# A softmax whose shift runs on ScalarE and whose exponential is taken after the transpose

## The chip, the cores and the metric

One core of a Trainium2 chip runs the whole program. The metric is the device time in microseconds (us), the median of three runs. Five engines work side by side and meet through semaphores: TensorE (PE, with its weight loads as PEld), VectorE (DVE), ScalarE (ACT), GpSimd (POOL) and SyncE (SP), which here only issues DMAs. Each engine takes its instructions in the order in which they are written.

## The reference

128 sequences of 128 rows of width 256 go through one gated block: cross-attention with 16 heads of width 16, then a feed-forward part whose activations are quantised per row.

```python
q, k, v = heads(layernorm(x) @ Wq.T + bq), heads(ctx @ Wk.T + bk), heads(ctx @ Wv.T + bv)
scores  = q @ k.T / sqrt(16)                 # per head, 128 x 128, masked above the diagonal
weights = softmax(scores, axis=-1)
x = x + tanh(g_xattn) * ((weights @ v) @ Wo.T + bo)
x = x + tanh(g_ffn) * bitlinear(silu(bitlinear(layernorm(x), w_gate)) * bitlinear(layernorm(x), w_up), w_down)
```

The change concerns the softmax alone: exp(score - row maximum) in 16 heads, and its transposition, since the product with v needs the keys on the partitions.

## The kernel before, in words

A tile is one sequence. The loop runs over pairs of sequences, each pair in two sections, `c.s == 0` (the even tile) and `c.s == 1` (the odd tile). A section works on four tiles at once, in four stages: attention of tile t, output projection of t-1 (`outp`), feed-forward of t-2 (`ffn`), down projection of t-3 (`down`); beside them the inputs of the next pair are projected (`proj`: k in the even section, q and v in the odd one). Each engine has its own `body(c)`, in which the order of its work is written out by hand for the two sections; `walk` calls it for 67 pairs of sections, of which 62 have every stage. `c.tile(n)` and `c.pair(n)` are the semaphore values of n tiles or pairs back.

Attention runs in two halves of eight heads. Half 0 lives in PSUM banks 0 and 1 (`S_B[0]`), half 1 in banks 2 and 3 (`S_B[1]`), each 128 queries by 1024 columns (8 heads of 128 keys). For each half of a tile:

- `scores` (TensorE, L499 to L510): six matmuls of 512 columns write the masked scores. They wait for `p_ok` of the tile before.
- `top` (VectorE, L845 to L851): a row maximum per head, negated, into `row_max`.
- Half 0: `shift` (VectorE, L853 to L857) adds `row_max` to the eight heads in one instruction and writes `prob` in SBUF; `exp` (ScalarE, L706 to L712) then takes the exponential of the 1024 columns in SBUF, in place.
- Half 1: `exp` (ScalarE, L714 to L719) takes the exponential straight out of PSUM, one instruction per head, with the head's `row_max` as bias.
- `probs_t` (TensorE, L512 to L516): eight transposes of `prob` back into the same banks.
- `probs_out` (ScalarE, L721 to L725): one copy of 1024 columns from PSUM to `prob_t` in SBUF, which releases `p_ok`.
- `values` (TensorE, L518 to L528): 16 matmuls with v; v has a column of ones, so that the sum of each row's exponentials comes with them. `out_natural` (L530, L859) transposes the result back and divides by that sum.

Other work that shares the engines and that the steps of the prediction name: the hidden transposes (L611) and ScalarE's `h_t` out of them (L768); ScalarE's `o_t` (L736) and VectorE's rest of it; the two gate/up halves (TensorE L597 to L609, where the second waits for `h_ok[0]`), ScalarE's `tanh` for each (L727 to L732), VectorE's `gu` and `h` (`gated`, L868 to L876); the output projection (L542 to L552); VectorE's `y` (L944); ScalarE's bias of k or q (L750) and `q_high` (L757); the maximum over the hidden row (L919). ScalarE's order in the odd section is `exp(1)`, `tanh(0)`, `exp(0)`, q, `probs_out(0)`, `tanh(1)`, `probs_out(1)`; in the even one `exp(0)`, `tanh(0)`, `exp(1)`, `probs_out(0)`, `tanh(1)`, k, `probs_out(1)`.

Of the kernel before, what the change touches and what calls it, by code (L numbers as in the profile page):

```python
# [12 lines left out]
P = 128  # L13
# [11 lines left out]
def flamingo_block(nc, x, ctx_in, g_x, g_f, wq, bq, wk, bk, wv, bv, wo, bo, w_gate, w_up, w_down, out):  # L25
# [15 lines left out]
    with es:  # L41
# [59 lines left out]
        prob = sb("prob", [P, HEADS, P])  # L101
# [256 lines left out]
        s_sub = sem("s_sub")  # L358
        s_exp = [sem("s_exp0"), sem("s_exp1")]
# [85 lines left out]
        with nc.Block() as block:  # L445
# [52 lines left out]
            def _(pe):  # L498
# [13 lines left out]
                def probs_t(c, half):  # L512
                    pe.wait_ge(s_exp[half], c.tile(0))
                    for n in range(HPC):
                        last = nc.tensor.transpose(S_B[half][:, n * P:(n + 1) * P], prob[:, HPC * half + n, :], ident[:, :])  # L515
                    last.then_inc(p_tr[half], 1)  # L516
# [117 lines left out]
                def body(c):  # L634
                    if c.s == 0:
# [18 lines left out]
                        if c.attn:  # L654
                            probs_t(c, 0)
# [6 lines left out]
                        if c.attn:  # L662
                            probs_t(c, 1)
# [5 lines left out]
                    else:  # L669
# [20 lines left out]
                        if c.attn:  # L690
                            probs_t(c, 1)
                            probs_t(c, 0)
# [12 lines left out]
            def _(act):  # L705
                def exp(c, half):  # L706
                    if half == 0:

                        act.wait_ge(s_sub, c.tile(0))
                        v = prob[:, 0:HPC, :]  # L710
                        nc.scalar.activation(v, v, ACT.Exp).then_inc(s_exp[0], 1)  # L711
                        return  # L712

                    act.wait_ge(s_max[1], c.tile(0))  # L714
                    wait(act, p_tr[1], c.tile(1))
                    for n in range(HPC):
                        last = nc.scalar.activation(prob[:, HPC + n, :], S_B[1][:, n * P:(n + 1) * P], ACT.Exp,  # L717
                                                    bias=row_max[:, HPC + n:HPC + n + 1])
                    last.then_inc(s_exp[1], 1)  # L719

                def probs_out(c, half):  # L721
                    act.wait_ge(p_tr[half], c.tile(0))
                    wait(act, pv_mm[half], c.tile(1))
                    nc.scalar.copy(prob_t[:, HPC * half:HPC * (half + 1), :].rearrange("p h k -> p (h k)"),  # L724
                                   S_B[half]).then_inc(p_ok[half], 1)  # L725
# [60 lines left out]
                def body(c):  # L786
                    if c.s == 0:
# [8 lines left out]
                        if c.attn:  # L796
                            exp(c, 0)
                        if c.ffn:
                            tanh(c, 0)
                        if c.attn:  # L800
                            exp(c, 1)
                            probs_out(c, 0)
# [4 lines left out]
                        if c.attn:  # L807
                            probs_out(c, 1)
# [335 lines left out]
```

## Time and profile before

| | |
|---|---|
| median of 3 runs | 1931.26 us (1930.18 to 1932.64) |
| the profiled execution, its own time | 1932.1 us |
| its span, first to last instruction | 1930.4 us |
| TensorE, matmuls | 1747.9 us busy, 91% |
| TensorE, weight loads | 1396.7 us, 72% |
| VectorE | 1658.1 us, 86%, 3609 instructions |
| ScalarE | 1434.1 us, 74%, 2897 instructions |
| GpSimd | 1053.1 us, 55% |
| TensorE's granted clock, mean | 0.99 of full speed |
| DMA | 91.22 MB, 47 GB/s |

Busy time is the union of an engine's instructions, so a share of 91% still has small gaps. A timeline line gives start, duration, engine, line of the kernel, operation, output <- input, the number of merged instructions, and in brackets the idle time of the engine before it with what ended it. In a group line "us, mean ns | idle before" is the busy total, the mean duration of one, and the idle time just before the group. Instructions of one engine overlap a little: the next starts before the recorded end of the one before it.

### The profile page before, as it was taken

To read this page: it belongs to the slowest core of one execution; us is meant where nothing else is said; L and a number is where in the kernel's file an instruction comes from. 1 tells how busy PE (TensorE), PEld (TensorE's weight loads), DVE (VectorE), ACT (ScalarE), POOL (GpSimd) and SP (SyncE) were. 2 spreads that over 40 slices of the span, in tenths; PEclk is the share of its full clock that TensorE was granted. 3 is DMA by queue.
4 is the path that set the end of the run, shared out by engine and by line. 5 is a ranking of instruction groups with operands and counts; after the bars stand their busy time and mean duration, and the time that the engine had idled before them with its cause. 6 is when DMAs were issued, how large, how long until landed. Compare 5 with 4: busy or idle time off the path is not lost. (4 is left out here: it accounts for less than half of the span.)

```text
span 1930.4 us, 46249 instructions
## 1 busy us (share of the span) xinstructions
PE 1747.9 (91%) x15430; PEld 1396.7 (72%) x15430; DVE 1658.1 (86%) x3609; ACT 1434.1 (74%) x2897; POOL 1053.1 (55%) x1623
## 2 busy tenths in 40 slices
PE   3799999999999999999999999999999999999984
PEld 2677777777777777777777777777777777777762
DVE  4588988988988888888898898898898898898884
ACT  3577777787777787777777777777777777778772
POOL 4455555556556556555555555555555555655641
PEclk9999999999999999999999999999999999999996
DMA  3222122122122122122122222222212212212210
GB/s 106 45 53 44 43 53 46 42 55 49 37 56 48 37 57 48 38 55 48 40 52 48 43 50 50 44 47 53 42 46 53 43 45 53 50 38 56 48 20 11
DMA packets 131900, 91.22 MB, mean 47 GB/s; under 512 B 13521, under 2 KB 131409, under 8 KB 131665
## 3 DMA queue, kind: packets, MB, share of 16 engines
q1 hardware_dynamic: 130416, 88.13, 22.4%
q8 instruction: 126, 2.06, 0.4%
q14 instruction: 110, 0.89, 0.2%
q10 hardware_dynamic: 1248, 0.14, 0.1%
HBM read 37.88 MB, written 16.78 MB: 28 GB/s over the span
## 5 line engine op out<-in xcount | busy, mean ns | idle before, releaser
L507 PE MATMUL psum<-k_blk,q_t 128*128 128x512 f32 x1536 | 419.1, 408 | 1.2 <-DVE q_t L935 1.2
L1041 POOL TENSOR_SCALAR xc<-x,ln 128x256 f32<-128x256 f32 x128 | 61.3, 479 | 485.5 <-DVE ln L898 485.5
L849 DVE TENSOR_REDUCE row_max<-psum 128x8 f32<-128x1024 f32 x256 | 311.2, 1215 | 7.1 <-PE psum L507 6.9
L507 PEld LDWEIGHTS psum<-k_blk,q_t 128*128 128x128 f32 x1536 | 268.8, 188 | 62.1 <-issue 14.1
L717 ACT ACTIVATE prob<-psum,row_max 128x128 f32<-128x128 f32 x1024 | 277.4, 385 | 12.7 <-DVE row_max L849 12.6
L1064 POOL TENSOR_SCALAR hq<-h,sm 128x1024 f16<-128x1024 f32 x128 | 143.2, 1119 | 226.6 <-DVE sm L929 220.5
L724 ACT COPY prob_t<-psum 128x1024 f32<-128x1024 f32 x256 | 262.4, 1025 | 5.1 <-PE psum L515 1.4
L515 PE MATMUL psum<-ident,prob 128*128 128x128 f32 x2048 | 255.1, 273 | 4.4 <-ACT prob L711 3.9
L515 PEld LDWEIGHTS psum<-ident,prob 128*128 128x128 f32 x2048 | 228.8, 141 | 6.6 <-ACT prob L711 5.1
L732 ACT ACTIVATE th<-psum,sm 128x512 f32<-128x512 f32 x256 | 178.8, 698 | 14.9 <-PE psum L607 13.2
L872 DVE SCALAR_TENSOR_TENSOR gu<-th,psum 128x512 f32<-128x512 f32 x256 | 174.9, 683 | 10.9 <-ACT th L732 6.8
L876 DVE TENSOR_TENSOR h<-gu,psum 128x512 f32<-128x512 f32 x256 | 175.9, 687 | 8.8
L773 ACT COPY o_raw<-psum 128x512 f32<-128x512 f32 x128 | 75.1, 587 | 139.4 <-PE psum L526 139.4
L607 PE MATMUL psum<-wg_t,xq_t 128*128 128x512 f16 x512 | 155.0, 385 | 21.7 <-DVE h L876 20.5
L526 PE MATMUL psum<-prob_t,v_sb 128*32 128x128 f32 x4096 | 151.6, 277 | 19.0 <-ACT prob_t L724 19.0
L768 ACT ACTIVATE h_t<-psum 128x1024 f16<-128x1024 f16 x128 | 131.0, 1023 | 41.0 <-PE psum L614 39.6
L856 DVE TENSOR_TENSOR prob<-psum,row_max 128x1024 f32<-128x1024 f32 x128 | 155.6, 1216 | 2.2
L919 DVE TENSOR_REDUCE sm<-h 128x1 f32<-128x1024 f32 x128 | 155.5, 1215 | 2.2
L711 ACT ACTIVATE prob<-prob 128x1024 f32<-128x1024 f32 x128 | 139.2, 1087 | 20.9 <-DVE prob L856 20.9
L607 PE MATMUL psum<-wu_t,xq_t 128*128 128x512 f16 x512 | 153.7, 382 | 0.0
L624 PE MATMUL psum<-wd_t,h_t 128*128 128x256 f16 x1024 | 135.9, 277 | 18.3 <-ACT h_t L768 18.3
L526 PEld LDWEIGHTS psum<-prob_t,v_sb 128*32 128x32 f32 x4096 | 100.2, 109 | 68.3 <-ACT prob_t L724 35.5
(116 smaller groups left out, 3729.9 us busy)
## 6 DMA issues: line engine op xcount, KB each, us to landing
k_blk<-k_t SPq DMA_DIRECT2D x512, 64.0 KB, 2.4
c_in<-in_ctx SPq DMA_DIRECT2D x64, 256.0 KB
x_in<-in_x SPq DMA_DIRECT2D x64, 256.0 KB
out<-y SPq DMA_DIRECT2D x128, 128.0 KB
g_nat<-in_L_ffn_w_gate SPq DMA_DIRECT2D x1, 1024.0 KB, 10.5
g_nat<-in_L_ffn_w_up SPq DMA_DIRECT2D x1, 1024.0 KB, 12.8
g_nat<-in_L_ffn_w_down SPq DMA_DIRECT2D x1, 1024.0 KB, 14.4
w_nat<-in_L_xattn_Wq SPq DMA_DIRECT2D x1, 256.0 KB, 4.1
```

The source lines that it names most:

```text
L507: last = nc.tensor.matmul(dst, q_t[:, b, a, half, c.s, :], k_blk[:, w, half, c.s, 4 * b:4 * b + 4, :], start=n == 0, stop=n == len(TERMS) - 1)
L515: last = nc.tensor.transpose(S_B[half][:, n * P:(n + 1) * P], prob[:, HPC * half + n, :], ident[:, :])
L526: last = nc.tensor.matmul(B6[VW * j:VW * (j + 1), g * P:(g + 1) * P], v_sb[:, c.s, n, :], prob_t[:, n, :], start=True, stop=True)
L607: last = nc.tensor.matmul(dst, xq_t[:, ic, :], w[:, ic, half * HALF:(half + 1) * HALF], start=ic == 0, stop=ic == DC - 1)
L717: last = nc.scalar.activation(prob[:, HPC + n, :], S_B[1][:, n * P:(n + 1) * P], ACT.Exp, bias=row_max[:, HPC + n:HPC + n + 1])
L724: nc.scalar.copy(prob_t[:, HPC * half:HPC * (half + 1), :].rearrange("p h k -> p (h k)"), S_B[half]).then_inc(p_ok[half], 1)
L732: nc.scalar.activation(th[:, half, :], GATE, ACT.Tanh, scale=row(sm, c.s, G_FACTOR)).then_inc(th_ok[half], 1)
L849: nc.vector.tensor_reduce(out=row_max[:, HPC * half:HPC * (half + 1)], in_=S_B[half].rearrange("p (h k) -> p h k", k=P), axis=AX.X, op=ALU ...
L856: nc.vector.tensor_tensor(prob[:, 0:HPC, :], S_B[0].rearrange("p (h k) -> p h k", k=P), row_max[:, 0:HPC].unsqueeze(2).to_broadcast((P, HP ...
L872: nc.vector.scalar_tensor_tensor(out=gu[:, half, :], in0=th[:, half, :], scalar=1.0, in1=UP, op0=ALU.add, op1=ALU.mult).then_inc(gu_ok[hal ...
L876: nc.vector.tensor_tensor(h[:, half, :], gu[:, half, :], GATE, ALU.mult).then_inc(h_ok[half], 1)
L919: nc.vector.tensor_reduce(out=row(sm, t, H_MAX), in_=h[:, :, :].rearrange("p a b -> p (a b)"), axis=AX.X, op=ALU.max, apply_absolute_value ...
```

## The change

VectorE's add leaves, and ScalarE adds the row maximum in both halves, one Identity instruction per head with the head's `row_max` as bias, from PSUM into `s_low` (the former `prob`). TensorE transposes these shifted scores. The exponential is then the instruction that takes the transposed 1024 columns out of PSUM into `prob_t`, where a copy stood. ScalarE's order becomes, even section: shift 0, tanh 0, shift 1, exponential 0, tanh 1, k, exponential 1; odd section: shift 0, tanh 0, shift 1, q, `q_high`, exponential 0, tanh 1, exponential 1. In the odd section the halves were taken as 1, 0 and are now taken as 0, 1.

```diff
--- before.py
+++ after.py
@@ -98,7 +98,7 @@
         k_t = sb("k_t", [P, 2, DC, 2, P], F32R)
         k_blk = sb("k_blk", [P, 2, DC, 2, HPC, P], F32R)
         v_sb = sb("v_sb", [P, 2, HEADS, VW])
-        prob = sb("prob", [P, HEADS, P])
+        s_low = sb("s_low", [P, HEADS, P])
         prob_t = sb("prob_t", [P, HEADS, P])
         o_raw = sb("o_raw", [P, 4 * P])
         o_n = sb("o_n", [P, D])
@@ -355,8 +355,7 @@
 
         s_mm = [sem("s_mm0"), sem("s_mm1")]
         s_max = [sem("s_max0"), sem("s_max1")]
-        s_sub = sem("s_sub")
-        s_exp = [sem("s_exp0"), sem("s_exp1")]
+        s_sub = [sem("s_sub0"), sem("s_sub1")]
         p_tr = [sem("p_tr0"), sem("p_tr1")]
         p_ok = [sem("p_ok0"), sem("p_ok1")]
         pv_mm = [sem("pv_mm0"), sem("pv_mm1")]
@@ -509,10 +508,10 @@
                                                     start=n == 0, stop=n == len(TERMS) - 1)
                     last.then_inc(s_mm[half], 1)
 
-                def probs_t(c, half):
-                    pe.wait_ge(s_exp[half], c.tile(0))
+                def shifted_t(c, half):
+                    pe.wait_ge(s_sub[half], c.tile(0))
                     for n in range(HPC):
-                        last = nc.tensor.transpose(S_B[half][:, n * P:(n + 1) * P], prob[:, HPC * half + n, :], ident[:, :])
+                        last = nc.tensor.transpose(S_B[half][:, n * P:(n + 1) * P], s_low[:, HPC * half + n, :], ident[:, :])
                     last.then_inc(p_tr[half], 1)
 
                 def values(c, half):
@@ -652,7 +651,7 @@
                         if c.down:
                             down(c)
                         if c.attn:
-                            probs_t(c, 0)
+                            shifted_t(c, 0)
                         if c.outp:
                             out_proj(c)
                         if c.ffn:
@@ -660,7 +659,7 @@
                         if c.proj:
                             project_qk(c)
                         if c.attn:
-                            probs_t(c, 1)
+                            shifted_t(c, 1)
                         if c.next.attn:
                             scores(c.next, 0)
                         if c.attn:
@@ -688,8 +687,8 @@
                         if c.proj:
                             project_qk(c)
                         if c.attn:
-                            probs_t(c, 1)
-                            probs_t(c, 0)
+                            shifted_t(c, 0)
+                            shifted_t(c, 1)
                         if c.ffn:
                             gate_up(c, 1)
                         if c.proj:
@@ -703,26 +702,20 @@
 
             @block.scalar
             def _(act):
+                def shift(c, half):
+                    act.wait_ge(s_max[half], c.tile(0))
+                    wait(act, p_tr[half], c.tile(1))
+                    for n in range(HPC):
+                        at = HPC * half + n
+                        last = nc.scalar.activation(s_low[:, at, :], S_B[half][:, n * P:(n + 1) * P], ACT.Identity,
+                                                    bias=row_max[:, at:at + 1])
+                    last.then_inc(s_sub[half], 1)
+
                 def exp(c, half):
-                    if half == 0:
-
-                        act.wait_ge(s_sub, c.tile(0))
-                        v = prob[:, 0:HPC, :]
-                        nc.scalar.activation(v, v, ACT.Exp).then_inc(s_exp[0], 1)
-                        return
-
-                    act.wait_ge(s_max[1], c.tile(0))
-                    wait(act, p_tr[1], c.tile(1))
-                    for n in range(HPC):
-                        last = nc.scalar.activation(prob[:, HPC + n, :], S_B[1][:, n * P:(n + 1) * P], ACT.Exp,
-                                                    bias=row_max[:, HPC + n:HPC + n + 1])
-                    last.then_inc(s_exp[1], 1)
-
-                def probs_out(c, half):
                     act.wait_ge(p_tr[half], c.tile(0))
                     wait(act, pv_mm[half], c.tile(1))
-                    nc.scalar.copy(prob_t[:, HPC * half:HPC * (half + 1), :].rearrange("p h k -> p (h k)"),
-                                   S_B[half]).then_inc(p_ok[half], 1)
+                    nc.scalar.activation(prob_t[:, HPC * half:HPC * (half + 1), :].rearrange("p h k -> p (h k)"),
+                                         S_B[half], ACT.Exp).then_inc(p_ok[half], 1)
 
                 def tanh(c, half):
                     act.wait_ge(gu_mm[half], c.tile(2))
@@ -794,18 +787,18 @@
                         if c.outp:
                             out_t(c)
                         if c.attn:
+                            shift(c, 0)
+                        if c.ffn:
+                            tanh(c, 0)
+                        if c.attn:
+                            shift(c, 1)
                             exp(c, 0)
                         if c.ffn:
-                            tanh(c, 0)
+                            tanh(c, 1)
+                        if c.proj:
+                            project_qk(c)
                         if c.attn:
                             exp(c, 1)
-                            probs_out(c, 0)
-                        if c.ffn:
-                            tanh(c, 1)
-                        if c.proj:
-                            project_qk(c)
-                        if c.attn:
-                            probs_out(c, 1)
                             values(c)
                             keep_residual(c)
                     else:
@@ -818,20 +811,20 @@
                         if c.outp:
                             out_t(c)
                         if c.attn:
-                            exp(c, 1)
+                            shift(c, 0)
                         if c.ffn:
                             tanh(c, 0)
                         if c.attn:
-                            exp(c, 0)
+                            shift(c, 1)
                         if c.proj:
                             project_qk(c)
                             q_high(c)
                         if c.attn:
-                            probs_out(c, 0)
+                            exp(c, 0)
                         if c.ffn:
                             tanh(c, 1)
                         if c.attn:
-                            probs_out(c, 1)
+                            exp(c, 1)
                             values(c)
                         if c.proj:
                             project_v(c)
@@ -845,16 +838,10 @@
                 def top(c, half):
 
                     dve.wait_ge(s_mm[half], c.tile(0))
-                    wait(dve, s_exp[1] if half == 1 else s_sub, c.tile(1))
+                    wait(dve, s_sub[half], c.tile(1))
                     nc.vector.tensor_reduce(out=row_max[:, HPC * half:HPC * (half + 1)],
                                             in_=S_B[half].rearrange("p (h k) -> p h k", k=P), axis=AX.X,
                                             op=ALU.max, negate=True).then_inc(s_max[half], 1)
-
-                def shift(c):
-                    dve.wait_ge(s_max[0], c.tile(0))
-                    wait(dve, p_tr[0], c.tile(1))
-                    nc.vector.tensor_tensor(prob[:, 0:HPC, :], S_B[0].rearrange("p (h k) -> p h k", k=P),
-                                            row_max[:, 0:HPC].unsqueeze(2).to_broadcast((P, HPC, P)), ALU.add).then_inc(s_sub, 1)
 
                 def out_natural(c):
                     dve.wait_ge(on_tr, c.tile(1))
@@ -969,7 +956,6 @@
                         if c.proj:
                             norm_stats(c)
                         if c.attn:
-                            shift(c)
                             top(c, 1)
                         if c.outp:
                             out_t(c)
@@ -990,7 +976,6 @@
                     else:
                         if c.attn:
                             top(c, 0)
-                            shift(c)
                         if c.outp:
                             out_natural(c)
                         if c.attn:
```

## Rows read from the trace of the kernel before

**Rows 1.** Busy time by stage: window, us, busy (instructions) per engine, clock, DMA

```profile
999.90:1028.60 28.70, 26.87 (x240) 21.56 (x240) 25.54 (x57) 22.16 (x45) 16.24 (x25) 1.00 0.24 47
```

**Rows 2.** Waits of TensorE over the span: us in total, times, longest

```profile
PE psum L607 <- DVE h L876: 20.5, 65, 2.2
PE psum L526 <- ACT prob_t L724: 19.0, 66, 0.8
```

**Rows 3.** Timeline, even tile of a steady pair: start, duration, engine, line

```profile
999.94 0.64 PE L526 MATMUL psum<-prob_t,v_sb 128*32 128x128 f32 x16 [0.28 <-ACT prob_t L724]
...
1003.27 1.21 DVE L849 TENSOR_REDUCE row_max<-psum 128x8 f32<-128x1024 f32 x1
...
1005.64 0.37 ACT L736 CAST o_t<-psum 128x256 fp32r<-128x256 f32 x1
...
1007.26 0.67 ACT L732 ACTIVATE th<-psum,sm 128x512 f32<-128x512 f32 x1
...
1007.72 1.04 PE L515 MATMUL psum<-ident,prob 128*128 128x128 f32 x8
...
1007.92 0.48 DVE L944 SCALAR_TENSOR_TENSOR y<-psum,sm,x 128x256 f32<-128x256 f32 x1 [0.20 <-PE psum L624]
1008.32 0.68 DVE L872 SCALAR_TENSOR_TENSOR gu<-th,psum 128x512 f32<-128x512 f32 x1
...
1008.55 0.94 PE L549 MATMUL psum<-w_t,o_t 128*128 128x256 f32 x6
...
1009.78 0.61 PE L607 MATMUL psum<-wg_t,xq_t 128*128 128x512 f16 x2 [0.28 <-DVE h L876]
...
1010.86 0.69 ACT L732 ACTIVATE th<-psum,sm 128x512 f32<-128x512 f32 x1
```

**Rows 4.** Timeline, odd tile of the same pair

```profile
1018.59 1.02 ACT L768 ACTIVATE h_t<-psum 128x1024 f16<-128x1024 f16 x1 [0.25 <-PE psum L614]
...
1019.51 0.37 ACT L736 CAST o_t<-psum 128x256 fp32r<-128x256 f32 x1
...
1020.07 2.17 ACT L717 ACTIVATE prob<-psum,row_max 128x128 f32<-128x128 f32 x8 [0.19 <-DVE row_max L849]
...
1022.08 0.74 ACT L732 ACTIVATE th<-psum,sm 128x512 f32<-128x512 f32 x1
...
1023.77 0.84 ACT L750 ACTIVATE q_f<-psum,bq_c 128x256 f32<-128x256 f32 x2
...
1024.64 1.26 ACT L757 CAST q_t<-q_f 64x512 fp32r<-64x512 f32 x2
...
1025.92 1.02 ACT L724 COPY prob_t<-psum 128x1024 f32<-128x1024 f32 x1
...
1026.97 0.69 ACT L732 ACTIVATE th<-psum,sm 128x512 f32<-128x512 f32 x1
...
1027.55 1.00 ACT L724 COPY prob_t<-psum 128x1024 f32<-128x1024 f32 x1
...
1028.61 0.64 PE L526 MATMUL psum<-prob_t,v_sb 128*32 128x128 f32 x16 [0.28 <-ACT prob_t L724]
```

**Rows 5.** Groups of instructions by line and form: busy us, mean ns, idle before

```profile
L717 ACT ACTIVATE prob<-psum,row_max 128x128 f32<-128x128 f32 x1024 | 277.4, 385 | 12.7 <-DVE row_max L849 12.6
...
L724 ACT COPY prob_t<-psum 128x1024 f32<-128x1024 f32 x256 | 262.4, 1025 | 5.1 <-PE psum L515 1.4
...
L856 DVE TENSOR_TENSOR prob<-psum,row_max 128x1024 f32<-128x1024 f32 x128 | 155.6, 1216 | 2.2
...
L711 ACT ACTIVATE prob<-prob 128x1024 f32<-128x1024 f32 x128 | 139.2, 1087 | 20.9 <-DVE prob L856 20.9
```

**Rows 6.** Timeline, VectorE and TensorE at the start of the odd tile

```profile
1015.81 1.22 DVE L849 TENSOR_REDUCE row_max<-psum 128x8 f32<-128x1024 f32 x1
...
1017.51 0.60 PE L533 MATMUL psum<-ident,o_raw 128*128 128x128 f32 x4
...
1018.20 0.25 DVE L862 RECIPROCAL row_rcp<-psum 128x16 f32<-128x16 f32 x1
```

More of the change, by code:

```diff
@@ L820, in body @@
                         if c.attn:
-                            exp(c, 1)
+                            shift(c, 0)
                         if c.ffn:
@@ L824, in body @@
                         if c.attn:
-                            exp(c, 0)
+                            shift(c, 1)
                         if c.proj:
@@ L829, in body @@
                         if c.attn:
-                            probs_out(c, 0)
+                            exp(c, 0)
                         if c.ffn:
@@ L833, in body @@
                         if c.attn:
-                            probs_out(c, 1)
+                            exp(c, 1)
                             values(c)
```

## The prediction

> **What bounds the kernel now.** I read the stage table of one steady pair of sequences first: in a window of 28.70 us TensorE is busy for 26.87, VectorE for 25.54, ScalarE for 22.16 and GpSimd for 16.24; TensorE's clock is at its full 2.4 GHz level (granted 1.00) [rows 1]. So TensorE sets the pace, with 1.8 us of idle time per pair, and a change can gain no more than that unless it removes TensorE work; this one removes none (16 score transposes per tile before and after). Then the waits: two of TensorE's gaps end with an engine that the change touches. It waits 20.5 us in all, 65 times, for VectorE's `h` before the second gate/up half, and 19.0 us, 66 times, for ScalarE's `prob_t` before the value matmuls [rows 2], 0.3 us each time. Last the timeline of that pair, even tile [rows 3] and odd tile [rows 4]; the pair lasts 28.67 us, from one launch of the last value matmuls at 999.94 to the next at 1028.61. What it shows: the engine with the largest share is not the one that ends every stage. In the second half of the odd tile ScalarE works without a break from the exponential of 1020.07 to the copy that ends at 1028.55, and TensorE's last value matmuls start 0.06 us after it [rows 4].
>
> **What the change moves.** Per tile, VectorE loses one add of 1.22 us (L856) and ScalarE loses one exponential of 1.09 us (L711); the exponential of 8 x 128 columns with a bias column (L717, 8 in 2.17 us) becomes an Identity of the same form; ScalarE gains a second set of those eight; both PSUM copies (L724) become exponentials [rows 5]. Instructions on ScalarE: 11 per tile become 18. No DMA and no GpSimd instruction is added or moved. In the odd tile the order of the halves is swapped, for ScalarE's shifts and TensorE's transposes alike.
>
> Prices. **Eight shifts**: 2.17 us, since L717 is the same form (128x128 out of PSUM, a bias column), with another function. That Identity is not much cheaper: two Identities of 256 columns with a bias column start 0.37 us apart (0.84 us for both, less 0.47), and eight exponentials of 128 columns 0.255 us apart ((2.17 - 0.385) / 7) [rows 4, 5]. A column costs 0.855 ns by the 1024-column copy against the 0.37 us, 256-column one ((1025 - 370) / 768) [rows 4, 5], so 128 columns fewer make the Identity's step 0.37 - 0.11 = 0.26 us. Ends: 2.07 and 2.27 us. **Exponential of 1024 columns out of PSUM**: not in the trace; ends are the PSUM copy, 1.025, and the exponential out of SBUF, 1.087 [rows 5]. I take 1.04, nearer the copy, since source and columns are the same and only the function differs.
>
> The Trainium skill, "ScalarE: Activation LUTs", section "What ACT_TABLE_LOAD costs", gives an ACTIVATE with a bias pointer about 280 ns + 0.833 ns per column, and an overlap of 93 ns between neighbours. For 128 columns that is 387 ns, and the trace agrees with 385; for eight, though, it is 2.44 us where the trace has 2.17, and the sum below would become +1.78 us per pair instead of +0.97. I follow the trace. The Trainium skill, the same page's section "Rules for kernel authors", puts an add on VectorE, not ScalarE, which speaks against this change; the trace agrees (1.22 us there, 2.17 here).
>
> **VectorE's gain.** 1.22 us per tile goes from an engine that has 3.1 us idle per pair. In the odd tile the add is followed by L862, which starts at 1018.20 and also needs the transposes of L533, which end at 1018.11: without the add it could start about 0.05 us sooner at most [rows 6]. In the even tile the following row maximum waits for the score matmuls anyway. I cost the removal at nothing; what covers it is TensorE's own order.
>
> **Even tile.** ScalarE issues the next instruction about 0.10 us before the recorded end of its predecessor (1018.59 + 1.02 - 0.10 = 1019.51) [rows 4], and 0.16 us before the end of a set of eight (1020.07 + 2.17 - 0.16 = 1022.08). After `o_t` (1005.64, 0.37 us) the first shift starts at 1005.91 and ends at 1008.08, because the row maximum, done at 1004.48, is long there. The tanh behind it starts at 1007.92 instead of 1007.26 and ends at 1008.59. VectorE's L872 started at 1008.32, held by L944 until 1008.40; now it is held by the tanh and starts at 1008.62 (a hand-over of 0.03): **+0.30 us**. Then `h` and the second gate/up matmuls, already waiting for it at 1009.78, go to 1010.08. The transposes on the way start at 1008.14 instead of 1007.72, and the output projection behind them ends at about 1009.91 instead of 1009.49: under 1010.08, so the tanh decides [rows 3]. The shift of half 1 (1008.49 to 1010.66) and exponential 0 (from 1010.50) are done before TensorE needs them; the second tanh starts at about 1011.57. From there TensorE has no break until its hidden transposes of the odd tile, and the +0.30 travels on.
>
> **Odd tile.** `h_t` waits for those transposes, so `o_t` is at 1019.51 + 0.30 = 1019.81, and then ScalarE never waits: shift 0 starts at 1020.08; tanh 0 at 1022.09 (+2.01); shift 1 at 1022.67 (+0.58, as 1026.97 to 1027.55), ends 1024.84; q bias at 1024.68; q high at 1025.55 (+0.87, as 1023.77 to 1024.64); exponential 0 at 1026.83 (+1.28, as 1024.64 to 1025.92); tanh 1 at 1027.90 (+1.05 for the copy, +0.02 for the function); exponential 1 at 1028.48, ends 1029.52. TensorE's last value matmuls follow 0.06 later, at 1029.58 instead of 1028.61 [rows 4]: **+0.97 us for the pair**, 0.30 of the even and 0.67 of the odd tile. On the way the transposes of half 1, which can't start before shift 1 ends at 1024.84, may hold TensorE for a moment; that is swallowed by the later wait. The wait for `prob_t` grows from 0.28 us to at most 0.28 + 0.67 = 0.95.
>
> **Sum.** 62 pairs run with all stages in, 62 x 0.97 = +60 us. In the first and last pair the feed-forward or the projections are missing and ScalarE has room; from row maximum to `p_ok` the work of a half is no longer than before (2.17 against 1.22 + 1.09), so I add nothing. The profiled execution took 1932.1 us with a span of 1930.4; it becomes 1992. It stood 0.8 us above the median of the three runs, 1931.26, so I predict **1991 us**, +3.1%. Each 0.1 us on a set of eight counts three times per pair (once even, twice odd), 19 us in all; the exponential's far end, 1.087, adds 0.05 twice, 6 us.
>
> **Rivals.**
> - *The even tile's delay does not come, or the shifts are a little cheap.* With sets at 2.07 us, +0.67 x 62 = 42: 1973 us. For it: Identity is another function than the one measured. Against: the 0.26 us step above. Chance 0.13.
> - *VectorE becomes late behind the second tanh.* In the even tile tanh 1 slips by 0.71 (1010.86 as it was, 1011.57 now), with it `gu`, `h`, the hidden maximum, and the odd tile's first row maximum, L849, from 1015.81 to 1016.52. If this reached TensorE in full in place of 0.30, the pair would grow by 1.38 us: +86, 2017 us. Against: that row maximum ends at 1017.74, and L862 behind it must wait for transposes that end at 1018.41, so 0.67 us of slack is left; the add's removal is what makes the room [rows 6]. Chance 0.09.
> - *Not slower: Identity is cheap enough.* The place is ScalarE's chain in the odd tile. It decides at a set of 1.83 us (0.67 = 2 x 0.335 saved), a step of 0.206 us instead of 0.255. Below 1.70 us the old 0.28 us wait for `prob_t` vanishes as well, and then -0.28 x 62 = -17: 1914 us. Against: the Identities of L750 show no such speed. Chance 0.07 for this side together.
> - That the change does not do what it says is excluded by its text: the add is gone from VectorE's order, and both halves take the same path.
>
> **Chances and range.** A measurement of this kernel can tell about 0.2% (4 us) from no change. Forecast 0.71, smaller loss 0.13, VectorE late 0.09, not slower 0.07, of which faster 0.05 and within the bound 0.02. So slower by over 0.2%: 0.93. The forecast's own range is 1979 to 1999 (sets of 2.12 to 2.19 us, exponentials of 1.025 to 1.087). With the smaller loss and half of the larger one the range becomes 1972 to 2008.
>
> **What would show it.** Right: in the changed profile, ScalarE's sets of eight at 2.1 to 2.2 us, twice per tile; 1024-column exponentials out of PSUM at 1.03 to 1.09 us; TensorE's wait for `prob_t` at 0.7 to 0.95 us in each pair, some 50 us in all, and its wait for `h` at 0.3 to 0.5; VectorE's idle time up by over 3 us per pair; a pair of 29.6 us. Wrong: a pair of 28.7 us or less; no growth of the wait for `prob_t`; a new wait of TensorE for `o_n`, `hq` or `xq`, which would mean that VectorE's chain counts; or Identities 0.2 us apart.

## The result and the profile after

| | before | after |
|---|---|---|
| median | 1931.4 us | 1991.45 us (1990.44 to 1993.63) |
| ratio to before, 95% interval | | 1.0311 (1.0298 to 1.0323) |
| span of the profiled execution | 1930.4 us | 1990.2 us |
| a pair, median between launches of L533/L532 two apart | 28.70 us | 29.68 us |
| of it from the even tile's launch to the odd one's, and back | 15.52, 13.18 us | 15.77, 13.91 us |
| instructions of ScalarE, of VectorE | 2897, 3609 | 3793, 3481 |

The change costs 3.1%: 60 us, or 0.98 us for each of the 62 full pairs. Line numbers after are one lower on TensorE's side and 7 to 15 lower behind it (L525 is the old L526, L514 the old L515, L606 the old L607; L710 is the shift, L717 the exponential out of PSUM, L725 the tanh, L842 the row maximum, L849 the old L862).

The stage table of a steady pair after, with the columns of [rows 1]:

```profile
999.90:1029.60 29.70, 27.20 (x240) 21.52 (x240) 23.57 (x55) 24.05 (x60) 16.40 (x25) 1.00 0.22 46
```

Against [rows 1] ScalarE is 1.9 us busier and VectorE 2.0 us less. TensorE's idle time in the window is 2.50 us, of 1.83 before. VectorE's goes from 3.2 to 6.1 us. The engine that was relieved is not the one that the pair waits for.

TensorE's waits over the span, after:

```profile
PE psum L525 <- ACT prob_t L717: 48.8, 65, 1.1
PE psum L565 <- ACT xq_t L776: 35.1, 62, 0.6
PE psum L538 <- DVE o_n L852: 25.3, 65, 1.0
...
PE psum L514 <- ACT s_low L710: 20.1, 66, 1.6
PE psum L606 <- DVE h L863: 16.2, 64, 2.2
```

Against [rows 2] the wait for `prob_t` grew by 30 us and a wait for the shifted scores appeared, 20 us; the wait for `h` did not grow, it fell by 4. The three waits that grew most all end with ScalarE (the third is the one for `h_t`, 18.3 to 22.3 us over the span); the one for VectorE's `o_n` fell from 29.8 to 25.3.

The timeline of the even tile after, to be laid beside [rows 3] (this pair starts 0.10 us later, 1000.04 for 999.94):

```profile
1000.04 0.65 PE L525 MATMUL psum<-prob_t,v_sb 128*32 128x128 f32 x16 [0.75 <-ACT prob_t L717]
...
1005.66 0.37 ACT L729 CAST o_t<-psum 128x256 fp32r<-128x256 f32 x1
...
1005.91 2.19 ACT L710 ACTIVATE s_low<-psum,row_max 128x128 f32<-128x128 f32 x8
...
1007.92 0.76 ACT L725 ACTIVATE th<-psum,sm 128x512 f32<-128x512 f32 x1
...
1008.15 1.09 PE L514 MATMUL psum<-ident,s_low 128*128 128x128 f32 x8 [0.26 <-ACT s_low L710]
...
1008.71 0.69 DVE L859 SCALAR_TENSOR_TENSOR gu<-th,psum 128x512 f32<-128x512 f32 x1 [0.29 <-ACT th L725]
...
1010.18 0.60 PE L606 MATMUL psum<-wg_t,xq_t 128*128 128x512 f16 x2 [0.22 <-DVE h L863]
```

The shift starts when `o_t` is out of the way, at 1005.91, and the tanh follows at 1007.92, where it was at 1007.26. The transposes wait 0.26 us for the shift, `gu` 0.29 us for the tanh, and the second gate/up half starts at 1010.18, or 1010.08 without the offset, 0.30 us later than before. The offset is not constant, though: at the hidden transposes it has shrunk to 0.02 us (L613 at 1004.09, L614 before at 1004.07), so between them and the gate/up half the even tile loses 0.38 us.

The odd tile after, beside [rows 4]:

```profile
1019.91 0.37 ACT L729 CAST o_t<-psum 128x256 fp32r<-128x256 f32 x1
...
1020.16 2.19 ACT L710 ACTIVATE s_low<-psum,row_max 128x128 f32<-128x128 f32 x8
...
1022.17 0.76 ACT L725 ACTIVATE th<-psum,sm 128x512 f32<-128x512 f32 x1
...
1022.74 2.25 ACT L710 ACTIVATE s_low<-psum,row_max 128x128 f32<-128x128 f32 x8
...
1024.74 0.99 ACT L743 ACTIVATE q_f<-psum,bq_c 128x256 f32<-128x256 f32 x2
...
1025.76 1.26 ACT L750 CAST q_t<-q_f 64x512 fp32r<-64x512 f32 x2
...
1027.04 1.03 ACT L717 ACTIVATE prob_t<-psum 128x1024 f32<-128x1024 f32 x1
...
1028.09 0.69 ACT L725 ACTIVATE th<-psum,sm 128x512 f32<-128x512 f32 x1
...
1028.68 1.01 ACT L717 ACTIVATE prob_t<-psum 128x1024 f32<-128x1024 f32 x1
...
1029.75 0.65 PE L525 MATMUL psum<-prob_t,v_sb 128*32 128x128 f32 x16 [0.76 <-ACT prob_t L717]
```

ScalarE has no idle time in this stretch. Its q bias starts at 1024.74 where TensorE's projection was ready at 1024.14; in [rows 4] it started at 1023.77. Everything behind it is late, and TensorE waits 0.76 us for the last `prob_t`, 0.28 before.

The groups of instructions that the change made, after:

```profile
L710 ACT ACTIVATE s_low<-psum,row_max 128x128 f32<-128x128 f32 x2048 | 567.6, 439 | 0.1
...
L717 ACT ACTIVATE prob_t<-psum 128x1024 f32<-128x1024 f32 x256 | 271.4, 1061 | 3.7
...
L725 ACT ACTIVATE th<-psum,sm 128x512 f32<-128x512 f32 x256 | 194.9, 761 | 15.7 <-PE psum L606 14.1
```

### The profile page after: what moved, and what is told of

Its sections match the earlier page's. It is cut to its first block and busy times, and to the rows that moved or that the text cites. A ratio compares the mean times of both kernels' runs of the same rounds, so it can differ in the third digit from the quotient of the medians.

```text
span 1990.2 us, 47017 instructions
## 1 busy us (share of the span) xinstructions
PE 1765.1 (89%) x15430; PEld 1392.2 (70%) x15430; DVE 1527.0 (77%) x3481; ACT 1555.7 (78%) x3793; POOL 1063.8 (53%) x1623
## 5 line engine op out<-in xcount | busy, mean ns | idle before, releaser
L710 ACT ACTIVATE s_low<-psum,row_max 128x128 f32<-128x128 f32 x2048 | 567.6, 439 | 0.1
L842 DVE TENSOR_REDUCE row_max<-psum 128x8 f32<-128x1024 f32 x256 | 311.6, 1217 | 64.4 <-PE psum L506 64.3
L514 PE MATMUL psum<-ident,s_low 128*128 128x128 f32 x2048 | 272.0, 276 | 21.8 <-ACT s_low L710 20.1
L717 ACT ACTIVATE prob_t<-psum 128x1024 f32<-128x1024 f32 x256 | 271.4, 1061 | 3.7
L514 PEld LDWEIGHTS psum<-ident,s_low 128*128 128x128 f32 x2048 | 224.7, 141 | 55.1 <-ACT s_low L710 54.8
L725 ACT ACTIVATE th<-psum,sm 128x512 f32<-128x512 f32 x256 | 194.9, 761 | 15.7 <-PE psum L606 14.1
L525 PE MATMUL psum<-prob_t,v_sb 128*32 128x128 f32 x4096 | 151.6, 277 | 48.8 <-ACT prob_t L717 48.8
L606 PE MATMUL psum<-wg_t,xq_t 128*128 128x512 f16 x512 | 155.0, 385 | 17.4 <-DVE h L863 16.2
L525 PEld LDWEIGHTS psum<-prob_t,v_sb 128*32 128x32 f32 x4096 | 100.1, 109 | 98.0 <-ACT prob_t L717 65.3
L623 PE MATMUL psum<-wd_t,h_t 128*128 128x256 f16 x1024 | 136.0, 277 | 22.3 <-ACT h_t L761 22.3
L606 PE MATMUL psum<-wu_t,xq_t 128*128 128x512 f16 x512 | 153.5, 382 | 0.0
L623 PEld LDWEIGHTS psum<-wd_t,h_t 128*128 128x128 f16 x1024 | 95.9, 99 | 62.5 <-ACT h_t L761 37.7
L922 DVE TENSOR_TENSOR q_t<-q_f,q_t 64x512 fp32r<-64x512 f32 x128 | 99.2, 775 | 37.4 <-ACT q_t L750 35.2
```

Of the source, the lines that this page charges most:

```text
L525: last = nc.tensor.matmul(B6[VW * j:VW * (j + 1), g * P:(g + 1) * P], v_sb[:, c.s, n, :], prob_t[:, n, :], start=True, stop=True)
L606: last = nc.tensor.matmul(dst, xq_t[:, ic, :], w[:, ic, half * HALF:(half + 1) * HALF], start=ic == 0, stop=ic == DC - 1)
L623: last = nc.tensor.matmul(DOWN, h_t[:, k * P:(k + 1) * P], wd_t[:, k, :], start=k == 0, stop=k == IC - 1)
L710: last = nc.scalar.activation(s_low[:, at, :], S_B[half][:, n * P:(n + 1) * P], ACT.Identity, bias=row_max[:, at:at + 1])
L717: nc.scalar.activation(prob_t[:, HPC * half:HPC * (half + 1), :].rearrange("p h k -> p (h k)"), S_B[half], ACT.Exp).then_inc(p_ok[half], 1)
L725: nc.scalar.activation(th[:, half, :], GATE, ACT.Tanh, scale=row(sm, c.s, G_FACTOR)).then_inc(th_ok[half], 1)
```

## The experiments

Eight of them price a part of the change, three look for a faster version. Each is compared with the kernel before on its own chip; where a difference counts, I take ratios.

**1. half1_only: the later exponential, by itself.**

```diff
-    last = nc.scalar.activation(prob[:, HPC + n, :], S_B[1][...], ACT.Exp, bias=...)
+    last = nc.scalar.activation(prob[:, HPC + n, :], S_B[1][...], ACT.Identity, bias=...)
...
-    nc.scalar.copy(prob_t[...], S_B[half])
+    nc.scalar.activation(prob_t[...], S_B[half], ACT.Exp if half == 1 else ACT.Copy)
```

> The kernel before, with half 1 alone changed: its eight ScalarE instructions per tile become Identity, and its exponential is taken on the way out of PSUM, in place of the copy. Half 0 stays as before. My theory: an Identity of 128 columns with a bias column costs what the exponential did (a set of eight 2.17 us, as after, 2.19), and an exponential of 1024 columns out of PSUM costs what the copy did (1.02 to 1.03 us in the trace of after, where it does not overlap a set). So nothing moves: 1931 us, within 4. Rival, the function itself costs: an exponential out of PSUM as dear as the one out of SBUF (1.09 us) would lengthen the odd tile's last ScalarE instruction by 0.06 us, 62 times, 1935 us; a cheaper Identity would bring the time below 1925.

Measured: 1931.62 us, ratio 1.0002 (0.9993 to 1.0011). ScalarE's groups:

```profile
L717 ACT ACTIVATE prob<-psum,row_max 128x128 f32<-128x128 f32 x1024 | 277.5, 386 | 12.7 <-DVE row_max L849 12.7
L724 ACT ACTIVATE prob_t<-psum 128x1024 f32<-128x1024 f32 x256 | 265.5, 1037 | 5.1 <-PE psum L515 1.4
```

Identity takes 386 ns as the exponential did (385, [rows 5]), and the mixed group of copies and exponentials 1037 ns for 1025. Moving the exponential of half 1 behind the transpose costs nothing.

**2. dve_add: the exponential behind the transpose in both halves, VectorE keeps the add.**

```diff
 # half1_only, and for half 0:
-    nc.scalar.activation(v, v, ACT.Exp).then_inc(s_exp[0], 1)      # exp(c, 0), gone
-    pe.wait_ge(s_exp[half], c.tile(0))
+    pe.wait_ge(s_exp[1] if half == 1 else s_sub, c.tile(0))
-    ... ACT.Exp if half == 1 else ACT.Copy)
+    ... ACT.Exp)
```

> The same as half1_only, and half 0 too is exponentiated on the way out; but the row maximum of half 0 is still added by VectorE, in one instruction, as in the kernel before, and ScalarE's exponential of 1.09 us per tile goes. ScalarE's and TensorE's order stay those of before. My theory (ScalarE's chain in the odd tile ends the pair, and the loss came from the second set of eight): ScalarE is done 1.0 us sooner in the odd tile, so TensorE's 0.28 us wait for prob_t goes, and nothing else on the path: 62 x 0.28 = 17 us, 1914 us (1910 to 1920). The even tile keeps its wait for h, since VectorE's y comes before it. Rival, taking the exponential after the transpose is itself what costs (a later release of the banks): slower than 1931 us.

Measured: 1931.77 us, ratio 1.0001 (0.9992 to 1.0010). ScalarE does 1.09 us less per tile and the time is the same. My forecast of a 17 us gain fell. The odd tile of this kernel, ScalarE and the last value matmuls:

```profile
1020.06 2.17 ACT L710 ACTIVATE prob<-psum,row_max 128x128 f32<-128x128 f32 x8 [0.18 <-DVE row_max L838]
...
1022.08 0.74 ACT L725 ACTIVATE th<-psum,sm 128x512 f32<-128x512 f32 x1
...
1023.78 0.84 ACT L743 ACTIVATE q_f<-psum,bq_c 128x256 f32<-128x256 f32 x2 [0.97 <-PE psum L579]
...
1025.93 1.03 ACT L717 ACTIVATE prob_t<-psum 128x1024 f32<-128x1024 f32 x1
...
1027.57 1.02 ACT L717 ACTIVATE prob_t<-psum 128x1024 f32<-128x1024 f32 x1
...
1028.64 0.65 PE L526 MATMUL psum<-prob_t,v_sb 128*32 128x128 f32 x16 [0.30 <-ACT prob_t L717]
```

The q bias has 0.97 us of idle time before it and starts at 1023.78, as in [rows 4]: it waits for TensorE's projection, which ends at 1023.75. In the kernel before, ScalarE's exponential of half 0 and TensorE's projection ended within 0.03 us of each other, at 1023.76 and 1023.73:

```profile
1022.17 1.56 PE L579 MATMUL psum<-xn_t,w_t 128*128 128x256 f32 x12
...
1022.65 1.11 ACT L711 ACTIVATE prob<-prob 128x1024 f32<-128x1024 f32 x1
```

So its row looked like one chain without a break, while in its first half ScalarE was only level with TensorE: shortening that half gains nothing, and lengthening it by more than what little slack there is costs. What sets the last wait is the stretch from the q bias on (q, q high, exponential, tanh, exponential), whose length this change hardly touches. With both results, the step from before to dve_add costs nothing, and the whole loss comes with taking the add from VectorE to ScalarE (and with the new order of the halves, which experiment 4 prices).

**3. cheap_even, cheap_odd, cheap_both: the set of eight priced tile by tile.** One Identity of 1024 columns in place of each set of eight (the row maximum is not added in those tiles).

```diff
+    if c.s == 0:        # cheap_even; 1 for cheap_odd; no condition for cheap_both
+        nc.scalar.activation(s_low[:, HPC * half:HPC * (half + 1), :]..., S_B[half], ACT.Identity)
+        return
     for n in range(HPC):
```

> The changed kernel, in whose even tiles each set of eight shifts is one Identity of 1024 columns (1.0 us in place of 2.2). It leaves out the addition of the row maximum there. By my theory the even tile's share of the loss is 0.30 us per pair and goes, while 1.2 us per set are saved: the tanh is then no longer late and VectorE's y holds gu again, TensorE's 0.26 us wait for s_low goes and its wait for h is 0.28 again. 62 x 0.30 = 19: 1973 us (1969 to 1978). Rival, ScalarE's whole time counts: 2 x 1.2 x 62 = 149 us, 1843 us.

> The same in the odd tiles alone. ScalarE saves 2.3 us there. My theory as corrected by dve_add (in which ScalarE was done with its shifts 1 us early and the pair was no shorter, since its q bias then waits for TensorE's q projection and TensorE's last wait for prob_t stays 0.3 us): the odd tile returns to its state before the change and no further, 0.67 us per pair less, and the even tile's 0.30 stays: 1950 us (1945 to 1955). My theory as it was, in which a shorter ScalarE chain also removes the old 0.28 us wait: 1932 us.

> Both of the former: one Identity of 1024 columns in place of every set of eight, no addition of the row maximum. If the loss is the two shares and the rest of the change costs nothing (exponential on the way out, order of halves, the add gone from VectorE): 1931 us again (1928 to 1935), although ScalarE has 4.6 us per pair less to do than in the changed kernel and VectorE 2.4 less than before. Rival, a part of the loss is in the new order or in the later exponential: over 1937 us; a real gain from the relieved engines: under 1926 us.

Measured: cheap_even 1967.1 us, 1.0185 (1.0171 to 1.0199); cheap_odd 1955.4 us, 1.0124 (1.0110 to 1.0138); cheap_both 1930.1 us, 0.9991 (0.9982 to 1.0000). Pairs: 29.31, 29.08, 28.69 us. The two savings, 24 and 36 us, add up to the 60 us of the loss, and with both the changed kernel is back where the old one was. TensorE's waits in cheap_even, cheap_odd and cheap_both, in this order:

```profile
PE psum L525 <- ACT prob_t L721: 48.0, 64, 1.1
...
PE psum L606 <- DVE h L867: 20.5, 65, 2.2
```

```profile
PE psum L525 <- ACT prob_t L721: 19.1, 63, 1.1
PE psum L514 <- ACT s_low L714: 18.1, 64, 1.7
PE psum L606 <- DVE h L867: 17.0, 65, 2.2
```

```profile
PE psum L525 <- ACT prob_t L714: 19.1, 63, 1.1
...
PE psum L606 <- DVE h L860: 21.0, 65, 2.2
```

Each cure takes its own symptom: in the odd tile the `prob_t` wait falls from 48.8 to 19.1 us, in the even one the `s_low` wait falls out of the list and `h` is back at 20.5. That cheap_odd stops at 29.08 and not lower bears out what dve_add taught.

The single shares missed my bands by a little: even 0.37 us per pair, not 0.30, odd 0.60, not 0.67. The even share is larger because the tanh behind a set of eight takes longer than I had it (see the part on the sum below). The odd one is smaller because of a third wait, that of the weight load for the hidden transposes on GpSimd's `hq`, over the span; before, after, cheap_odd:

```profile
PEld psum L614 <- POOL hq L1064: 21.7, 63, 6.5
```

```profile
PEld psum L613 <- POOL hq L1049: 9.9, 6, 6.2
```

```profile
PEld psum L613 <- POOL hq L1053: 19.5, 52, 6.5
```

In the kernel before TensorE waits for `hq` in 63 places; after, TensorE is late by its own, and the wait is gone (6 left); cheap_odd brings it back 52 times (cheap_both 53, cheap_even 6). In steady pairs, from L532 to the matmuls of L613 it is 1.96 us after and 2.05 in cheap_odd (2.07 before). The odd tile's delay hides 0.1 us of the next even tile's work, and a removal of the former gives that back: the odd tile's own section gets 0.7 us shorter in cheap_odd (13.91 to 13.20), the next even one 0.1 us longer (15.77 to 15.87). The order in which the shares are taken doesn't matter: the even one is 0.37 us taken first (29.68 to 29.31) and 0.39 taken second (29.08 to 28.69), the odd one 0.60 and 0.62.

**4. odd_swap: the order of the halves in the odd tile as it was.**

```diff
-    shifted_t(c, 0)
-    shifted_t(c, 1)
+    shifted_t(c, 1)
+    shifted_t(c, 0)
... # and on ScalarE
-    shift(c, 0) ... tanh(c, 0) ... shift(c, 1)
+    shift(c, 1) ... tanh(c, 0) ... shift(c, 0)
```

> The changed kernel with the halves of the odd tile in the order 1, 0 again, for ScalarE's shifts and TensorE's transposes. My theory (ScalarE never waits in the odd tile after o_t, so that whatever delays its first shift delays the pair): the first shift then needs the row maximum of half 1, which ends at 1020.39 where ScalarE is free at 1020.16, and starts some 0.27 us later: 62 x 0.27 = 17 us, 2008 us (2003 to 2012). Rival, the order is indifferent because TensorE or VectorE ends the pair: 1991 us, within 4.

Measured: 2006.9 us, 1.0391 (1.0375 to 1.0407), within the forecast; a pair is 29.93 us, 0.25 longer. ScalarE's odd chain passes a later start straight on. The swap that the change made is worth about 15 us; without it the loss would be 76.

**5. dve_dummy and dve_odd_add: what VectorE's relief is worth.**

```diff
+    def dummy(c):                                    # dve_dummy, both tiles
+        nc.vector.tensor_tensor(spare, g_nat[:, 0, 0:1024]..., bo_eff[:, 0:HPC]..., ALU.add)
 # dve_odd_add, odd tile alone:
+        dve.wait_ge(s_max[0], c.tile(0))
+        dve.wait_ge(s_mm[1], c.tile(0))
+        nc.vector.tensor_tensor(spare, S_B[1]..., row_max[:, 0:HPC]..., ALU.add)
```

> The changed kernel with VectorE's 1.2 us given back: at the places where the shift stood, an add of the same 1024 columns on constants, which nobody waits for. If VectorE's relief is worth nothing, as I costed it: 1991 us, within 4. What the trace of after makes likelier: in the even tile nothing (0.9 us idle before the next row maximum, of 1.2, and slack behind it); in the odd tile VectorE has 0.83 us idle before L849, so o_n comes some 0.4 us later, its transposes and then ScalarE's o_t slip by 0.1 to 0.2 us, and ScalarE's chain with them: 1997 to 2004 us. Rival, VectorE's busy time counts in full: 2 x 1.2 x 62 = 149 us, 2140 us.

> The changed kernel with the very add that was removed (1024 columns out of PSUM plus the row maximum column, 1.22 us) put back on VectorE in the odd tile alone, at its old place between the first row maximum and L849; its result goes to a tile that nobody reads. dve_dummy left this open: its add read two SBUF operands, took 1.39 us, and GpSimd's small instruction beside it took 1.11 us in place of 0.26, after which TensorE's q projection waited 0.53 us for the split of xn. Theory by the trace of after: the row maximum ends at 1017.72, the add at 1018.9, L849 starts 0.3 us later than its 1018.55, o_n and its transposes too, and ScalarE's o_t slips by some 0.1 us: 62 x 0.1 = 6 us, 1997 us (1993 to 2002). If VectorE's relief is worth nothing: 1991, within 2. If what dve_dummy lost is VectorE's time and not GpSimd's: 2010.

Measured: dve_dummy 2010.8 us, 1.0410 (1.0395 to 1.0424); dve_odd_add 2009.7 us, 1.0394 (1.0377 to 1.0412), a pair 29.93 us. Both missed my bands. The second has an add of the real form (it reads the bank of half 1 and waits for those scores, which cost it 2.5 us in four places and nothing elsewhere), GpSimd is undisturbed, and it is one add per pair; still it costs 16 us (1.0394 less 1.0311), where I had expected 6; the 2010 us of its last rival, VectorE's time and not GpSimd's, is what came. Its waits of TensorE and its odd tile:

```profile
PE psum L539 <- DVE o_n L859: 47.3, 66, 1.1
PE psum L515 <- ACT s_low L711: 36.3, 126, 1.7
```

```profile
1024.39 1.21 DVE L843 TENSOR_REDUCE row_max<-psum 128x8 f32<-128x1024 f32 x1
...
1025.65 1.22 DVE L850 TENSOR_TENSOR spare<-psum,row_max 128x1024 f32<-128x1024 f32 x1
...
1026.79 0.25 DVE L856 RECIPROCAL row_rcp<-psum 128x16 f32<-128x16 f32 x1
...
1027.55 0.44 PE L539 MATMUL psum<-ident,o_n 128*128 128x128 f32 x2 [0.69 <-DVE o_n L859]
...
1028.02 0.37 ACT L730 CAST o_t<-psum 128x256 fp32r<-128x256 f32 x1
```

Behind the late first maximum (1024.39 to 1025.60) the add ends at 1026.87, the reciprocal (L856 of this kernel) and `o_n` follow, the wait for `o_n` goes from 25.3 to 47.3 us, and ScalarE's `o_t` starts 2.21 us after the launch of L533 (1025.81) instead of 2.00 (1017.91 to 1019.91). From there the odd chain carries the 0.2 us to the end, and TensorE meets it as a second wait for `s_low` in each pair (36.3 us for 20.1). So the removed add was worth 0.25 us per pair in the changed kernel. That it is worth this only because the second tanh has made VectorE late is read from the rows and no run separates it: with the add, the first maximum starts 1.42 us ahead of L533 here and 1.70 ahead in the kernel before (1015.81 and 1017.51, [rows 6]), where `o_t` still comes 2.00 us after L533 (1019.51, [rows 4]).

**6. early_half0 and scores_first: two tries at a faster version.**

```diff
 # early_half0, on dve_add, odd tile: TensorE           ScalarE
+    probs_t(c, 0)      # ahead of out_proj             # tanh 0, exponential 0, q, q_high,
     out_proj(c); project_qk(c); probs_t(c, 1)          # exponential 1, tanh 1
 # scores_first_add (on dve_add), scores_first_before (on before), TensorE, even tile
     quant_t(c)
+    scores(c, 1)
     inputs_t(c); out_t(c); hidden_t(c)
-    scores(c, 1)
```

> dve_add (VectorE adds for half 0, the exponential on the way out in both halves) with a new order in the odd tile: TensorE transposes half 0 ahead of the output projection, ScalarE takes exponential 0 ahead of q and exponential 1 ahead of the second tanh. In dve_add ScalarE is idle for 0.97 us before q, waiting for TensorE, and then does q, q high, exponential 0, tanh, exponential 1 in a row. If that row sets TensorE's last wait of the pair (0.30 us for prob_t): moving one exponential ahead of q removes it, 62 x 0.29 = 18: 1914 us (1910 to 1918). Rival, the time only moves on: the wait for prob_t goes and another wait of the pair (o_n, h_t, xq_t or h) grows by as much: 1931 us.

> dve_add with one step of TensorE's even tile moved: the scores of half 1 come right behind the transposes of xq, ahead of those of the inputs, of o_n and of the hidden row. They fill the 0.56 us in which TensorE waits for ScalarE's xq_t (the longest wait in every kernel here, 35 us in all), but what they overtake comes about 1 us later. Worked out by the timeline of dve_add: h_t ends at 1006.6 instead of 1005.7, the down projection starts at 1006.65 instead of 1006.84, y and gu some 0.2 us sooner, the second gate/up half 0.2 us sooner. My theory: since ScalarE has no exponential 0 in front of the tanh, the tanh (about 1006.8 to 1007.5) is still ready before y is, and the pair is 0.2 us shorter: 62 x 0.22 = 14, 1918 us (1910 to 1926). Rival, the overtaken steps cost as much as is filled: 1931 us or more.

> The same move in the kernel before, whose ScalarE has the exponential of 1.09 us between o_t and the tanh. If ScalarE's place in the even tile decides, the tanh comes at 1007.75 instead of 1007.26, ends at 1008.4, gu starts at 1008.45 instead of 1008.32, and the move gains nothing: +0.1 us per pair, 1938 us (1932 to 1944). Rival, ScalarE's exponential has slack there: 1918 us, as the other.

Measured: early_half0 1982.3 us, 1.0265 (1.0251 to 1.0279); scores_first_add 1958.6 us, 1.0141 (1.0126 to 1.0156); scores_first_before 1957.3 us, 1.0135 (1.0118 to 1.0152). All three forecasts failed. TensorE's waits in early_half0, then in scores_first_add:

```profile
PE psum L607 <- DVE h L867: 61.1, 128, 2.2
...
PE psum L614 <- POOL hq L1055: 26.1, 65, 5.6
```

```profile
PE psum L607 <- ACT h_t L761: 73.4, 63, 1.3
```

In early_half0 the `prob_t` wait did go, as planned. But the transposes push the output projection back by 0.8 us, VectorE takes the residual behind it ahead of `gu`, and the wait for `h` goes from 21 to 61 us. Most of the loss comes a tile later: the second `gu` and `h` of the odd tile, and with them `hq`, are late, the next hidden transposes start 2.63 us after the even tile's L533 instead of 2.05, and of the 0.83 us that the pair grows (28.70 to 29.53) 0.58 are in the even tile's section. In scores_first the fill-in cures the 35 us wait for `xq_t` and makes one of 73 us: the first gate/up half needs the bank that `h_t` is read from, and I had left `ht_ok` (L600) out of the walk. Nothing here beats the kernel before.

## Why the prediction was right

**The sum.** 1991 us forecast, 1991.45 measured; +0.97 us per pair forecast, +0.98 measured. The mechanism is the one forecast: in the even tile the first tanh comes behind a set of eight and holds `gu`, in the odd tile ScalarE's chain ends the pair, and nothing else costs. cheap_even, cheap_odd, cheap_both, half1_only and dve_add tested this.

That the sum agrees within 0.01 us is luck in part, since three terms were off and cancel.

- Even tile, 0.38 us and not 0.30. I gave the tanh the 0.67 us of its old place. Behind a set of eight it took 0.76, and [rows 4] had a tanh behind a set at 0.74 (1022.08), which I overlooked. The longer tanh is on the path: it ends at 1008.68 and `gu` starts at 1008.71. From the hidden transposes to the second gate/up half it is 5.71 us before (1004.07 to 1009.78) and 6.09 after (1004.09 to 1010.18).
- Odd tile, 0.73 us and not 0.67 (its section, 13.18 to 13.91): the q bias was dearer than I took it.
- Not in my walk at all: the late odd tile hides TensorE's wait for `hq`, 0.11 us of the next even tile (2.07 us from L533 to the hidden transposes before, 1.96 after).

Together 0.38 + 0.73 - 0.11 = 1.00, against 0.98 for the median pair. So the second gate/up half stands at its 1010.08 only because the gain at `hq` covers the term that I had too small; the last value matmuls, forecast at 1029.58, stand at 1029.65.

**Prices.** The 0.47 us in my estimate of the Identity's step is the mean record of one L750 (474 ns for q), which none of the rows that I named shows. A set of eight Identities: 2.17 forecast, 2.19 and 2.26 recorded; from one launch to the next instruction's 2.01 and 2.00 (1005.91 to 1007.92, 1022.74 to 1024.74), as before. The exponential out of PSUM: 1.04 forecast; 1.01 to 1.03 in the rows of the odd tile, so the near end was the right one (the mean of 1.06 holds records that begin inside that of a set). From the formula of the Trainium skill ("ScalarE: Activation LUTs", "What ACT_TABLE_LOAD costs") I had estimated 2.44 us for eight and +1.78 us per pair: the trace has 2.19 and +0.98, and its rows were the better guide for a chain of eight. The Trainium skill's advice to leave an add to VectorE (same page, "Rules for kernel authors"), which it gives with a bf16 rate, held here for fp32: the step from dve_add to the changed kernel is the add's move, and it costs 60 us.

**The step that was right for a reason I had half.** "I cost the removal at nothing." In the trace of before nothing follows from it, and the sum, which was walked with the add gone, needed no more. But the reason I gave, that TensorE's order covers it, holds for the old schedule alone: dve_odd_add shows 16 us, since (as the rows suggest) the changed kernel's tanh makes VectorE's first maximum of the odd tile late (I had worked out 0.7 us; it is 0.59, 1016.50 less the offset of 0.10, for 1015.81). Of the three possible ends of this (nothing, the rival's full 86 us, something between) the third came: the removal pays for a delay that the same change makes. The rival "VectorE becomes late" had its mechanism right, and the room of 0.67 us that I counted against it is what the add would have eaten.

**What I read wrongly.** "ScalarE works without a break", taken as the sign that ScalarE's whole odd chain ends the pair. dve_add shows two chains that met: ScalarE's from `o_t` to the exponential of half 0, and TensorE's up to the q projection, within 0.03 us. The forecast did not suffer, since it only lengthened the first. The other side would have: my "not slower" case, with 0.28 us per pair to gain from a cheap Identity and 1914 us, could not come; cheap_both has sets of 1.0 us and stays at 1930. Its floor was the old time.

**Where the waits showed.** I expected the wait for `prob_t` at 0.7 to 0.95 us (0.76, in all 48.8: right), VectorE's idle time up by over 3 us (2.97, at the edge), and the wait for `h` at 0.3 to 0.5. That one is wrong: it is 0.22 to 0.25 us, less than before, because TensorE is itself held by the wait for `s_low` ahead of it. The even tile's loss is there, under another name. The q bias came 0.1 us dearer than in my walk (1024.74 to 1025.76, 1.02 where I took 0.87), which the cheaper exponentials partly gave back.

## What to carry to other kernels

Work taken from the engine with the higher share pays only if that engine ends a wait; look for the stretches in which another engine runs without idle time, and price the moved work by each time such a stretch contains it (here three times per pair, though it runs four times). A chain without a break may only be level with another one: then longer costs in full and shorter gains nothing, and one kernel that shortens it tells the two apart. When a schedule is tuned by hand, a wait that is filled by moving a step ahead pays only if every semaphore of the overtaken steps, their banks' releases too, has been walked.

## What was not expected of the hardware

- VectorE's add on two SBUF operands of 1024 columns took 1.39 us (dve_dummy), on PSUM and a column 1.22 us (dve_odd_add). Beside the former a GpSimd instruction that takes 0.26 us was recorded with 1.11 us, beside the latter with 0.27 us:

```profile
1028.38 1.37 DVE L848 TENSOR_TENSOR spare<-g_nat,bo_eff 128x1024 f32<-128x1024 f32 x1
...
1028.77 1.11 POOL L1060 TENSOR_SCALAR sm<-sm,cst 128x1 f32<-128x1 f32 x1
```

```profile
1025.92 0.27 POOL L1061 TENSOR_SCALAR sm<-sm,cst 128x1 f32<-128x1 f32 x1
```

- Eight Identities in the changed kernel are recorded with 439 ns each, in half1_only with 386 ns, though launches and the time of a set hardly differ; the tanh behind a set is recorded longer too (0.76 for 0.67 us, and 0.74 in [rows 4]). Why stays open. For the next instruction of ScalarE it is overlap; for another engine it is time on the path, since `gu` starts 0.03 us after the recorded end of the tanh (1008.68, 1008.71).
